# Layer 1's spreads as 64-row products in pairs beside the scores, in a two-layer attention and expert kernel

## What is computed

```python
xn = _layernorm(x)
x = x + _L0_attn_ref(xn, u, v) + _L0_ffn_ref(xn, Wr, Wqkv, Wo)
xn = _layernorm(x)
x = x + _L1_attn_ref(xn, ...) + _L1_ffn_ref(xn, w_gate, w_up, w_down)

# layer 0, attention: 16 channels of rank 64
qz_u, qz_v = qz @ u.T * SCALE, qz @ v.T * SCALE
qh = sigmoid(einsum('bcsr,bctr->bcst', qz_u, qz_v))
message = (qh @ qz_v) @ u + (qh.T @ qz_u) @ v          # times SCALE
# layer 0, experts: top 64 tokens per expert and batch, attention over them, rows added back
# layer 1, attention: a linear attention with a hierarchical state
q, k, v = elu(x @ Wq) + 1, elu(x @ Wk) + 1, x @ Wv      # 64 wide
# per token t: leaf blocks += k_n v_n^T ; W_l += (UL^T k_left)(VR^T v_right)^T ; z += k
# y = leaf q + UL W VR^T q_right (top), UR W^T VL^T q_left (bottom) ; out = (y / (z.q)) @ Wo
# layer 1, ffn: (silu(x Wg) * (x Wu)) Wd
```

## Time and profile before

| | us |
|---|---|
| median of 3 runs | 1639.15 |
| lowest and highest | 1637.25, 1639.43 |
| the profiled execution | 1642.11 |
| its span, first to last instruction | 1640.3 |
| PE busy | 1523.1 |
| DVE busy | 868.0 |
| ACT busy | 770.4 |
| POOL busy | 56.5 |

### The profile page before, as it was taken

The page is one execution under the profiler, slowest core; times in us unless marked ns, Lnnn a source line. Parts: engine busy times, 40 slices in busy tenths (PEclk is TensorE's granted clock), DMA queues, the critical chain, the costliest instruction groups (busy, mean ns, idle before and its releaser), DMA issues.

```text
span 1640.3 us, 25098 instructions
## 1 busy us (share of the span) xinstructions
PE 1523.1 (93%) x8272; PEld 859.1 (52%) x8272; DVE 868.0 (53%) x1552; ACT 770.4 (47%) x1172; POOL 56.5 (3%) x45
## 2 busy tenths in 40 slices
PE   3699799999999999999999999999999999999977
PEld 1566455555555455555555455555555555545544
DVE  8767633355454554455544554555545554454546
ACT  1246455555454554455444554454445544454431
POOL 5100400000000000000000000000000000000000
PEclk8799799999999999999999999999999999999988
DMA  6002100000000000000000000000000000000000
GB/s 195 1 21 66 27 1 1 1 8 1 1 1 9 7 1 1 9 7 1 1 1 16 1 1 1 9 7 1 1 9 7 1 1 1 10 1 1 1 7 7
DMA packets 24095, 18.22 MB, mean 11 GB/s; under 512 B 1632, under 2 KB 22240, under 8 KB 23808
## 3 DMA queue, kind: packets, MB, share of 16 engines
q1 hardware_dynamic: 23600, 14.27, 3.1%
q0 software_dynamic: 336, 1.97, 0.3%
HBM read 12.03 MB, written 4.19 MB: 10 GB/s over the span
## 4 chain that ended last, share of the span: by engine, by line
issue 86%; PE 6%; DVE 5%; POOL 1%; ACT 1%; DMA 0%; SPq 0%; DVEq 0%; POOLq 0%; ACTq 0%
PE psum L1092 6%; DVE arena L816 0%; DVE arena L646 0%; DVE small L645 0%; DVE arena L822 0%; DVE upper L580 0%; DMA x_all<-in_x 0%; DVE upper L596 0%; DVE upper L707 0%; DVE upper L705 0%; ACT arena L927 0%; DVE upper L703 0%; DVE upper L714 0%; DVE upper L716 0%; DVE arena L814 0%
## 5 line engine op out<-in xcount | busy, mean ns | idle before, releaser
L1015 ACT ACTIVATE th_second<-psum 128x1024 f32<-128x1024 f32 x256 | 248.8, 1023 | 437.6 <-PE psum L1092 437.6
L1015 ACT ACTIVATE arena<-psum 128x1024 f32<-128x1024 f32 x258 | 250.5, 1025 | 191.4 <-PE psum L1092 175.6
L760 DVE TENSOR_SCALAR o_hl<-psum,sums 128x512 fp32r<-128x512 f32 x128 | 96.1, 751 | 378.8 <-PE psum L1092 378.7
L1092 PE MATMUL psum<-arena 128*64 128x512 f32 x1024 | 248.0, 605 | 0.0
L1092 PE MATMUL psum<-th_second,arena 128*64 128x512 f32 x1024 | 241.5, 592 | 0.0
L1092 PE MATMUL psum<-u_parts,v_parts 64*128 64x512 f32 x1548 | 216.1, 412 | 11.0 <-DVE sel_r L853 7.3
L1092 PE MATMUL psum<-v_parts,u_parts 64*128 64x512 f32 (+1 forms) x1568 | 220.6, 408 | 0.0
L1092 PEld LDWEIGHTS psum<-u_parts,v_parts 64*128 64x128 f32 x1548 | 137.6, 187 | 104.1 <-issue 74.2
L1092 PEld LDWEIGHTS psum<-v_parts,u_parts 64*128 64x128 f32 (+1 forms) x1568 | 141.1, 185 | 96.4 <-issue 73.3
L927 ACT ACTIVATE arena<-psum 128x512 f32<-128x512 f32 (+4 forms) x228 | 127.3, 590 | 114.0 <-PE psum L1092 48.2
L1092 PEld LDWEIGHTS psum<-th_second,arena 128*64 128x64 f32 x1024 | 73.5, 137 | 146.2 <-issue 144.2
(11 more groups left out here) (199 smaller groups left out, 1716.5 us busy)
## 6 DMA issues: line engine op xcount, KB each, us to landing
x_all<-in_x SPq DMA_DIRECT2D x4, 512.0 KB, 5.8
upper<-in_we SPq DMA_DIRECT2D x8, 256.0 KB, 2.7
expert_rows<-upper SPq DMA_DIRECT2D x16, 128.0 KB, 2.5
xn_s<-expert_rows SPq DMA_DIRECT2D x8, 256.0 KB, 2.8
out<-x_all SPq DMA_DIRECT2D x8, 256.0 KB, 2.5
arena<-in_e POOLq DMA_DIRECT2D x1, 1216.0 KB, 6.0
arena<-in_wi POOLq DMA_DIRECT2D x1, 576.0 KB, 6.5
uT_w<-in_uT SPq DMA_DIRECT2D x1, 512.0 KB, 6.6
```

Of the source, the lines that this page charges most:

```text
L760: nc.vector.tensor_scalar(o_hl[:, o, 0], o_bank[:], total, None, ALU.add).then_inc(s_oh, 1)
L1015: nc.scalar.activation(th_of(un), psum[:, at:at + 2], ACT.Tanh, scale=0.5 * FACTOR_SCALE ** 2).then_inc(s_th, 2)
L1092: return nc.tensor.matmul(out, lhsT, rhs, start=start, stop=stop)
```

## The change

It does four things.

1. k and q share one tile in natural layout (k on rows 0 to 63, q on 64 to 127) with a high and a low part (`kq_parts`), and v has the same (`val_parts`, v on both halves). Ea and Eb stand over Ed and Eb in `e_high` and `e_low`. A spread is now two (f < 2) or three passes of 64 rows: A and B on array rows 0 to 63, C and D on 64 to 127. `row_spread` issues the members of a group pass by pass, one beside the other.
2. The spreads are ordered in 15 groups (`ROW_GROUPS`); a group stands directly behind the first scores of a half (`ROWS_BEFORE`) or directly ahead of the second (`ROWS_BEHIND`). A group waits for all its banks first, and its members count as full when the whole group is. The gate and up steps move to halves 13, 14 and 15, the last of which now has gate, up, den, yo and down.
3. DVE takes the low parts of norm and v straight from PSUM; one ACT copy (xn2T) and some DVE splits go.
4. Early first pair: PE computes the first pair's products beside the last expert, ACT and DVE read them out and split them there, `split_rows(0)` comes before the experts, and POOL splits uT and vT during the last expert. POOL's work on E shrinks.

```diff
-L1_STEPS = [("back", 0), ("norm", 0), ("kq", 0), ("v", 0)]
-for _f in range(NF):
-    L1_STEPS += [("B", _f), ("A", _f), ("C", _f)] + ([("D", _f)] if _f >= 2 else [])
+ROW_GROUPS = [(("B", 0),), (("A", 0),), (("B", 1), ("C", 0)), (("A", 1),), (("B", 2), ("C", 1)), (("A", 2), ("C", 2))]
+for _f in range(3, NF):
+    ROW_GROUPS += [(("B", _f), ("D", _f - 1)), (("A", _f), ("C", _f))]
+ROW_GROUPS += [(("D", NF - 1),)]
+L1_STEPS = [("back", 0), ("norm", 0), ("kq", 0), ("v", 0)] + [s for group in ROW_GROUPS for s in group]
...
-L1_IN_HALF = [0, 1, 1, 2, 2, 4, 2, 4, 2, 4, 2, 4, 2, 4, 2, 3]
+ROWS_BEFORE = {4: 0, 5: 2, 6: 4, 7: 5, 8: 7, 9: 8, 10: 10, 11: 11, 12: 13, 13: 14}
+ROWS_BEHIND = {4: 1, 5: 3, 7: 6, 9: 9, 11: 12}
+FULL_STEPS = {1: [("back", 0)], 2: [("norm", 0)], 3: [("kq", 0), ("v", 0)], 13: [("gate", 0), ("up", 0)],
+              14: [("gate", 1), ("up", 1)], 15: [("gate", 2), ("up", 2), ("den", 0), ("yo", 0), ("down", 0)]}
...
-            def spread(bk, step, f):
-                at0 = E_AT[step] + f * P
-                src = {"A": k_stk, "B": vl_stk, "C": q_stk, "D": q_stk}[step]
-                ins = mm(bk[:], e_str[:, at0:at0 + P], src[:], True, f < 2)
-                if f >= 2:
-                    ins = mm(bk[:], e_swp[:, at0:at0 + P], src[:], False, True)
+            def row_spread(group, L, banks):
...
+                for n, (a, b) in enumerate(((0, 0), (0, 1), (1, 0))):
+                    for (kind, f), bk in zip(group, banks):
+                        last = 2 if f >= 2 else 1
+                        if n <= last:
+                            rows = slice(0, 64) if kind in "AB" else slice(64, 128)
...
+                            ins = mm(bk[:], (e_high, e_low)[a][rows, at0:at0 + P], (val_parts if kind == "B" else kq_parts)[b][rows],
+                                     n == 0, n == last)
...
+                elif kind == "norm":
+                    dve.wait_ge(s_xh, L + 1)
+                    nc.vector.tensor_tensor(xn2_hl[:, 1], bk[:], xn2_hl[:, 0], ALU.subtract).then_inc(s_ld, 1)
...
-                    nc.vector.tensor_copy(k_stk[0:64], kf32[0:64])
-                    link(nc.vector.tensor_copy(q_stk[64:128], kf32[64:128]))
-                    nc.vector.tensor_tensor(k_stk[64:128], kf32[0:64], k_stk[0:64], ALU.subtract).then_inc(s_stk, 1)
-                    nc.vector.tensor_tensor(q_stk[0:64], kf32[64:128], q_stk[64:128], ALU.subtract).then_inc(s_stk, 1)
+                    link(nc.vector.tensor_copy(kq_parts[0][:], kf32[:]))
+                    nc.vector.tensor_tensor(kq_parts[1][:], kf32[:], kq_parts[0][:], ALU.subtract).then_inc(s_stk, 1)
...
-            pool.wait_ge(s_ymv[0], 16 * E)
-            pool.wait_ge(s_ymv[1], 16 * E)
...
-            split_weights(((uT_w, uv_hl[0]), (vT_w, uv_hl[1])), 0)
+            pool.wait_ge(s_sm, E)
+            split_weights(((uT_w, uv_hl[0]),), 0)
+            pool.wait_ge(s_av, E)
+            split_weights(((vT_w, uv_hl[1]),), 1)
+            pool.wait_ge(s_ymv[0], 16 * E)
+            pool.wait_ge(s_ymv[1], 16 * E)
...
-            for k in range(1, 5):
-                if k == 3:
-                    pe.wait_ge(s_ys, E)
-                if k == 4:
-                    pe.wait_ge(s_prep_free, 1)
-                prep(-1, k, 0, 0, x_banks[(k - 1) % X_BANKS])
+            last = (E - 1, 1, E // 2 - 1, False)
+            prep(-1, 1, 0, 0, bank[0])
+            prep(-1, 2, 0, 0, bank[1])
+            probabilities_back(*last)
+            prep(-1, 3, 0, 0, bank[2])
+            attend(*last)
+            prep(-1, 4, 0, 0, bank[3])
+            expert_out(*last)
```

More of the change, by code:

```diff
@@ L137 @@
 for _h in range(HALVES):
-    X_ORDER += MIDDLE[_h] + [("y", r) for r in range(ROUNDS) if Y_AT[r] == _h]
+    X_ORDER += [s for work in MIDDLE[_h] for s in steps_of(work)] + [("y", r) for r in range(ROUNDS) if Y_AT[r] == _h]
 while len(X_ORDER) % X_BANKS:
@@ L267, in build @@
         qf, kf = take_upper(T), take_upper(T)
-        v_s, s1, ptT, avT = (take_upper(TB, P) for _ in range(4))
+        v_s, s1, ptT = (take_upper(TB, P) for _ in range(3))
+        at_upper[0] += 2 * P
+        avT = take_upper(TB, P)
         y_s = take_upper(2, TB, P)
-        nmax, rsum, rinv = take_upper(TB), take_upper(TB), take_upper(TB)
+        nmax, rsum, rinv = take(TB), take(TB), take(TB)
+        assert at[0] <= KEPT
         at_upper[0] = mark
@@ L295, in build @@
         gT = take(T)
-        xn2T, kmin, kexp, kf32, bs, bs6, ab, pre = (take(T) for _ in range(8))
+        kmin, kexp, kf32, bs, bs6, ab, pre = (take(T) for _ in range(7))
         y_sb, gated, tg = kmin, ab, kexp
@@ L511, in _ @@
             pool.tensor_scalar(wd[:], wi_v[:, 2].rearrange("p (h d) -> p h d", h=HC), W_SCALE, None, ALU.mult).then_inc(s_hi, 1)
[L512 to L518, removed]
+            half = NE_LOW // 2
+            for n in range(2):
+                at0 = n * NF * P + 2 * P
+                ins = pool.tensor_tensor(e_low[:, n * half:(n + 1) * half], e_raw[:, at0:at0 + half], e_high[:, at0:at0 + half], ALU.subtract)
             ins.then_inc(s_prep_w, 1)
-            pool.wait_ge(s_ymv[0], 16 * E)
-            pool.wait_ge(s_ymv[1], 16 * E)
             def split_weights(pairs, done):
@@ L728, in _ @@
             link(nc.vector.reciprocal(rinv[:], rsum[:]))
+            prep_v(-1, 0)
             expert_rows(E - 1, 1, E // 2 - 1)
[L731 to L744, removed]
             def add_g(i, j):
@@ L950, in _, with prep_raw @@
             lagged(fori_of(act), high_part, picked)
+            def prep_raw(g, k, raw, total, par, q, bk):
+                act.wait_ge(s_prep_full, prep_index(g, k) + 1)
+                if not (isinstance(g, int) and g < 0):
+                    act.wait_ge(s_us if k == 1 else s_vs_rdy, g + 1)
+                    act.wait_ge(s_prep_full, prep_index(g, 1))
+                if q is not None:
+                    act.wait_ge(s_oe, (q - 1) * 2)
+                nc.scalar.activation(raw[:], bk[:], ACT.Copy, accum_out=total[:, par:par + 1]).then_inc(s_prep_free, 1)
             def picked_rows(n):
@@ L961, in attended @@
                 copy(ptT[:].rearrange("p a m -> p (a m)"), bank[5][:]).then_inc(s_ptc, 1)
+                if isinstance(n, int) and n == E - 1:
+                    prep_raw(-1, 2, v_raw, sums[:, 0], 0, None, bank[1])
                 act.wait_ge(s_av, n + 1)
@@ L979, in expert @@
                     picked_rows(n + 1)
+                else:
+                    prep_raw(-1, 1, u_raw, sums[:, 1], 0, None, bank[0])
                 act.wait_ge(s_sm, n + 1)
@@ L1328, in l1 @@
                     pe.wait_ge(s_xn2, L + 1)
[L1329 to L1330 removed]
                 if kind == "kq":
[L1332 removed]
+                    wait_emptied(pe, ("norm", 0), L)
                 if kind == "down":
@@ L1407, in iteration @@
                             prep(g, PREP_K[kind], (j + 1) % PAIRS, i if j < PAIRS - 1 else i + 1, x_bank(work))
+                        elif kind == "rows":
+                            if second:
+                                for step in work[1]:
+                                    wait_bank(step, i, second)
+                                row_spread(work[1], L, [x_bank(step) for step in work[1]])
                         elif second:
```

190 lines of the change are left out of this document (101 added, 89 removed).

## The result

The changed kernel takes 1658.7 us as the median of 4 runs (1658.3 to 1659.6), the one before 1639.3 (1637.3 to 1641.0, 4 runs): ratio 1.012, 95% interval 1.0102 to 1.0137. It is slower by 19.4 us; the forecast said 11. The profiled execution lasted 1658.6, its span 1656.8, so the spans differ by 16.4 (before rounding). The other 2.9 are no change of the kernel: the profiled execution of before lay that much above its median, this one doesn't.

A forecast was written before the change was run, and what follows sets the result against it. PE's issue and waits were taken to bound the rounds. Seven rounds +32.1, top-k -3.0, start -8.7, round 0 -2.8 and tail -6.4 gave +11.2 on a median of 1639.15, about 1650 us; whole range 1639 to 1662, the forecast's own 1643 to 1658.

The forecast's parts named there:

- passes: Each round with layer 1: 41 slots of 0.233 us in place of 46 full passes, -1.16 a round.
- kq product's wait: Half 3: the wait behind a queued DVE subtraction goes, as DVE does it a half earlier from PSUM, -0.8 a round.
- B0's bank: Half 4: `pv` no longer waits for this bank because it uses another one, -0.65 a round.
- waits for ACT: Halves 5, 6, 9, 10: banks come free at S + 2.1 (S: first scores issued), after their next user comes up; +0.8 a round.
- DVE waits on C's bank: Halves 7, 8, 11, 12: PE waits while DVE multiplies A, scans and multiplies C; +5.9 a round.
- gate and up: Halves 13 and 15: PE waits for the bank of gate, before only once in half 13; +0.5 a round in all.
- The term that decides: The +5.9 a round of DVE waits in halves 7, 8, 11 and 12: 1.6 each in 7 and 11, 1.4 in 8 and 12.
- Ahead of the main phase: Everything up to the start of round 1: top-k -3.0, start of the main phase -8.7, round 0 -2.8.
- The scan of the top-k: Top-k's last DVE steps: with POOL done earlier the scan takes 1.22 and the steps 2.6 instead of 5.6, -3.0.
- `pj` waits of round 0: Round 0: waits for the bank of `pu` in pairs 2 to 7 remain in pair 7 alone, 5 x 0.56 = -2.8.
- Tail: After the last scores: B0 earlier, a shorter DVE chain and y rounds moved among the ffn products; -6.4, bounds -9 and -3.
- the lost start: Rival, main phase start: scores start early, but scatter_operands beside POOL or vT's parts hold PE as before; 1659, chance 0.15.

The follow-up runs named there:

- shifted order: The changed kernel with groups (C f-1, B f) and (D f-1, A f), so C and D stand a group behind A of their tile: 1607.8 us.
- stacked kernel: The kernel before with the early first pair, its 128-row stacked spreads kept but issued in the changed kernel's groups: 1688.3 us.

## Why the forecast had the sign and not the size

A round is split here into its slots (0.23 each) and the rest, half by half, as medians over rounds 1 to 7 of either trace:

| term of a round | forecast | measured | where |
|---|---|---|---|
| passes | -1.16 | -1.16 | counted: 41 slots for 46 |
| kq product's wait | -0.8 | -0.78 | half 3 |
| B0's bank | -0.65 | -0.67 | half 4 |
| waits for ACT | +0.8 | +0.64 | halves 5, 6, 9, 10 |
| DVE waits on C's bank | +5.9 | +6.26 | halves 7, 8, 11, 12: 1.70, 1.44, 1.68, 1.44 |
| gate and up | +0.5 | +0.54 | halves 13 and 15: -0.45, +0.98 |
| half 0 | none | +0.1 | mean; it lasts 9.7 to 10.5 in either kernel |
| sum | +4.6 | +4.9 | |
| slow stretches | none | +0.67 | three of 1.56 in seven rounds |

- **The term that decides** was right in place, releaser and nearly in size: `tv` has an excess of 0.48 and the group 1.56, `pj` 1.26, and the halves had lost a few tenths elsewhere before. The runs with an eighth of the scan and with two show that it is the scan; in the shifted order 6.0 of these 6.3 go. The second wait in half 3 stayed (1.04), as said. In half 5 a single wait grew to 0.94 of idle time, but shorter ones around it went, so the half is only 0.13 longer.
- **The step that was missing** is one that is not in the sum: that a stand of 1.4 can be followed by a stretch at 1.2 GHz. It makes 4.7 of the 7.2 by which the seven rounds missed; the other 2.5 are the DVE waits, which were 0.36 a round larger than forecast.
- **Pairs and the Trainium skill's rules.** The Trainium skill's "up to 2x" (TensorEngine Tiling (Array Packing), Theoretical Speedup) would have been 36 slots; lone passes keep a slot each, and it was 41. Its warning (PSUM Bottleneck) named the side of the loss, but the runs show one place in the order of read-out, not PSUM's rate.
- **Ahead of the main phase (-14.5 with round 0).** -16.1. The scan of the top-k takes 1.22, as forecast, though only 2.0 of it were left when the experts began. Scores start at 168.3 (169.6 forecast); PE then stands 2.69 for scatter_operands, where two DVE operations take 3.66 beside POOL's splits, so that rival's mechanism is real; the `weighted` products start at 189.5 instead of 202.3, 12.8 earlier where I had 11.7 with the top-k. Five of six `pj` waits of round 0 went, 0.68 each instead of 0.56.
- **Tail (-6.4).** -6.9; B0 stands 2.9 earlier in its chain (21.5 behind the last scores, 24.4 before).
- **From span to median.** The spans missed by 5.2: 7.2 in the rounds, less 1.6 ahead of them and 0.5 in the tail. 2.9 more of the miss of 8.7 is the profiled execution of before, which I subtracted as if after would share it; the rest is rounding.
- **What was luck.** 1658.7 lies above the 1643 to 1658 that my own forecast had, by little. The whole range reached up to 1662 for another reason, the lost start (1659), and the start was not lost but came 1.6 earlier than forecast. That this rival's number was met says nothing for it.

## What to carry to other kernels

Two products that are consumed one behind the other (here A, its scan, then C) must not hold banks of one small rotation in the same group: shift the second by a group; here even a scan done twice then cost the rounds nothing. Count a wait by when its bank is read out against the next user's place, engine by engine; that gave the six terms of a round to within 0.4 us from rows of the old kernel. And when PE will stand for 1.4 us or more in a dense phase, add to the wait a chance of losing as much again to the clock; stands of 1.10 were followed by no slow stretch here.

## What the hardware showed that I had not expected

- **PE starts 64-row matmuls out of their issue order.** With three passes per member issued in a row, the fourth started with the first (939.32) and the time stayed at 1606.8; with six narrow ones, the seventh started with the third and 18.5 us were lost. In these rows no matmul starts with more than three earlier ones still to come. The Trainium skill (TensorE: Matmul & The Clock Gate, Part 3: Packing small matmuls, The mechanism) says that matmuls start and end in program order and only weight loads are pulled ahead; for matmuls on different row halves these rows show otherwise, and the measurement decides.
- **The clock fell inside a dense phase.** Ahead of the group, an idle time of 1.40 was followed by some 1.5 us lost at 1.2 GHz in 3 of 14 places, one of 2.66 by 1.3 to 2.9 in 14 of 14; three of these rounds lost another 1.5 in half 8. In the stacked kernel it was 6 of 7 halves 7 and no half 11, at equal waits.
- **64-row passes of 256 columns cost half of those of 512** (0.12 and 0.23), with twice the weight loads.
